# First heads of attention through memory, half by half, and a rearranged projection on five engines

## The chip, the cores and the metric

One core of a Trainium2 chip runs the whole program. The metric is the device time of one execution in microseconds, lower is better; the time of a version is the median of several executions. The engines are TensorE (PE, with its weight loads as PEld), VectorE (DVE), ScalarE (ACT), GpSimd (POOL) and SyncE (SP), which issues most DMAs. SPq is its queue of issues.

## What is computed

The program computes a macaron block: half a mixture-of-experts layer, attention, and half a mixture-of-experts layer again, on x of 4 x 1024 tokens by 256 features. The attention has 16 heads of 16 features, is causal, and adds a second product to the scores:

```
Q, K, V = heads(norm(x))                       # 16 heads of 16
scores = Q K' / 4 + lambda * (tanh(Q) J) tanh(K)'
out    = softmax(causal(scores)) V
x      = x + out Wo' + bo
```

The change is in the part between the first mixture and the attention, in which Q, K, V and the tangent terms of the first sequence are projected.

## The kernel before

Attention works in 16 groups: 4 sequences by 4 groups of heads (GH = 4 heads of HD = 16 features). A group's operands are two tiles, `a_qp` and `a_kp`, of 96 partitions (rows) by 4 heads by 1024 tokens, and `a_vg`. The 96 rows hold high and low parts of Q, K and the tangent terms, so that one product of TensorE gives a nearly exact float32 score.

`project` prepares the first sequence, before `attend`. It has four stages `STAGES` = (half 0, g 0), (half 1, g 0), (half 0, g 1), (half 1, g 1); a half is 512 tokens (QC), g picks 128 of the 256 features (two groups of heads, "sides" 0 and 1). x_hi and x_lo are the high and low part of the transposed normalized x. Each stage n does, in an order that is written out by hand for every engine:

- TensorE `queries(n)` and `keys(n)`, 6 products of 512 columns each, and `tangents(n)`, 3 products, from tanh of the queries (tq_hi, tq_lo).
- ScalarE `queries_high`, `keys_high` (three activations each: high part, tanh, high part of tanh) and `tangents_high`.
- VectorE `queries_low`, `keys_low`, `tangents_low`; GpSimd makes the low part of tanh(K) in all stages (L1379), and of tanh(Q) in stages 2 and 3 (L1377). VectorE makes that of tanh(Q) in stages 0 and 1 (L1435).
- The results go to `pack[n]`, 8 arrays of 128 partitions by 512 tokens, in the order Q_HI, T_HI, Q_LO, T_LO, K_HI, TK_HI, K_LO, TK_LO.

SP issues in program order and stands still at each wait. For stages 0 and 1 `load_heads_directly` (L1271) copies each array of side 0 from the 64 partitions of `pack` to 16 partitions of `a_qp` or `a_kp`, 12 DMAs of 128 KB for a half, 24 in all, each released by the array that is made last. `send_pack` (L1202) writes 4 arrays of one side, 512 KB, to `packs` in memory; the side 1 arrays of both halves go there after the last direct load. Then follow the values, the packs of stage 2, and in `attend` the loads of group 1 from `packs` (L1250), its values (L1256) and the packs of stage 3.

In `attend`, `max_unit` (L2289) computes score blocks whose row maximum VectorE takes (L2060, L2063), 48 units for a group. The first waits for the first heads (`heads_in`, L2284), the first of group 1 for all loads of group 1 (`loaded[1]`, L2286). After six units TensorE turns the next half of x. After the second unit of group 1 VectorE reduces group 0's maxima; they are turned, negated and sent as row 97 of `a_qp` by a DMA, and only then the first `score` (L2323) can run.

In the same stage VectorE also does the statistics of x (`statistics`, L146: 4 + 4 + 8 + 16 tiles) and ScalarE the square roots, whose table of functions differs from that of tanh.

`keep_running` (L1268) are TensorE products without use, put where it would otherwise be idle.

Of the kernel before, what the change touches and what calls it, by code (L numbers as in the profile page):

```python
# [5 lines left out]
F32 = mybir.dt.float32  # L6
# [3 lines left out]
ALU = mybir.AluOpType  # L10
# [1267 lines left out]
Q_ROWS = {Q_HI: (0, 4 * HD), T_HI: (HD, 5 * HD), Q_LO: (2 * HD,), T_LO: (3 * HD,)}  # L1278
K_ROWS = {K_HI: (0, 2 * HD), TK_HI: (HD, 3 * HD), K_LO: (4 * HD,), TK_LO: (5 * HD,)}
DIRECT_LOADS = sum(len(to) for rows in (Q_ROWS, K_ROWS) for to in rows.values())  # L1280


def project(kit, c, passing, proj, sum_dram, packs, v_dram, group, group_in):
# [8 lines left out]
    with ExitStack() as ctx:  # L1292
# [5 lines left out]
        pack += [sb(f"pack{u}", [P, 8, QC], F32R)[:] for u in range(FIRST_LATER, n_stages)]  # L1298
        vals = [proj["vals"], sb("vals1", [P, NG, U, GH, HV])]
# [11 lines left out]
         y_done, high_q, high_k, high_t, low_q, low_k, low_pool, low_tq, low_t, t_done, v_done, v_read, side_out, late_out) = kit.sems_until(  # L1311
            passing, "q", "stats_done v_ready root_ready root_done deviated normed tposed x_hi_done x_lo_done w_high w_low "
            "y_done high_q high_k high_t low_q low_k low_pool low_tq low_t t_done v_done v_read side_out late_out")
# [8 lines left out]
        def sync(sp):  # L1322
# [15 lines left out]
            for n, (i, g) in enumerate(STAGES):  # L1338
                if n == n_stages - 1:
                    continue  # L1340
                if n == 2:
                    for half in range(FIRST_LATER):
                        sp.wait_ge(v_ready, 3 + (half + 1) * U)
                        send_values(sp, v_dram, vals[half], half, v_out[half])
                if g == 0:
                    sp.wait_ge(low_q, n + 1)
                    load_heads_directly(sp, group[0], pack[n], i, (Q_HI, Q_LO), Q_ROWS, landed)
                    sp.wait_ge(low_k, n + 1)
                    load_heads_directly(sp, group[1], pack[n], i, (K_HI, K_LO), K_ROWS, landed)
                    sp.wait_ge(low_pool, 2 + n + 1)  # L1350
                    load_heads_directly(sp, group[1], pack[n], i, (TK_HI, TK_LO), K_ROWS, landed)
                    sp.wait_ge(low_t, n + 1)
                    load_heads_directly(sp, group[0], pack[n], i, (T_HI, T_LO), Q_ROWS, landed)
                    if n == FIRST_LATER - 1:
                        for half in range(FIRST_LATER):
                            send_pack(sp, packs, pack[half], half, g, slice(K_HI, 8), side_out, (1,))
                            send_pack(sp, packs, pack[half], half, g, slice(0, K_HI), side_out, (1,))
                else:
                    sp.wait_ge(low_k, n + 1)
                    sp.wait_ge(low_pool, 2 + n + 1)  # L1360
                    send_pack(sp, packs, pack[n], i, g, slice(K_HI, 8), late_out)
                    sp.wait_ge(low_t, n + 1)
                    send_pack(sp, packs, pack[n], i, g, slice(0, K_HI), late_out)
        def gpsimd(pool):
# [9 lines left out]
            for n in range(n_stages):  # L1374
                if n >= FIRST_LATER:
                    pool.wait_ge(high_q, 3 * n + 3)
                    nc.gpsimd.tensor_tensor(tq_lo[n % 2][:], tq[n % 2][:], tq_hi[n % 2][:].bitcast(F32), ALU.subtract).then_inc(low_tq, 1)  # L1377
# [29 lines left out]
        def vector(dve):  # L1407
# [17 lines left out]

            def x_rest(i):
# [3 lines left out]

            def queries_low(n):
                i, g = STAGES[n]
                dve.wait_ge(high_q, 3 * n + 3)
                if n < FIRST_LATER:
                    nc.vector.tensor_tensor(tq_lo[n % 2][:], tq[n % 2][:], tq_hi[n % 2][:].bitcast(F32), ALU.subtract).then_inc(low_tq, 1)  # L1435
# [26 lines left out]
            norm(1)  # L1462
            dve.wait_ge(w_low, 3)
            queries_low(0)
            x_rest(1)
# [16 lines left out]
        def scalar(act):  # L1482
# [20 lines left out]
            def queries_high(n):  # L1503
# [4 lines left out]
                if n > 1:  # L1508
                    act.wait_ge(low_tq, n - 1)
# [31 lines left out]
            roots(act, U, BT, 2)  # L1541
            norm(1)
# [3 lines left out]
            x_high(1)  # L1546
# [11 lines left out]
        def tensor(pe):  # L1558
# [27 lines left out]
            def keys(n):  # L1586
                i, g = STAGES[n]
                if n == 0:
                    pe.wait_ge(w_low, 2)
                else:  # L1590
                    pe.wait_ge(low_q, n)
# [3 lines left out]
            def tangents(n):  # L1595
# [6 lines left out]
                pe.wait_ge(low_tq, n + 1)  # L1602
# [22 lines left out]
            transposes(1)  # L1625
            tangents(0)
            queries(1)
# [34 lines left out]
def attend(kit, c, proj, sum_dram, packs, v_dram, o_dram, inv_dram, wo_dram, bo_dram, group, group_in):  # L1662
# [18 lines left out]
    with ExitStack() as ctx:  # L1681
# [124 lines left out]
        def sync(sp):  # L1806
# [28 lines left out]
            sp.wait_ge(heads_in, FIRST_LATER * DIRECT_LOADS * 16)  # L1835
# [80 lines left out]
        def gpsimd(pool):  # L1916
# [6 lines left out]
            pool.wait_ge(heads_in, FIRST_LATER * DIRECT_LOADS * 16)  # L1923
# [291 lines left out]
        def tensor(pe):  # L2215
# [65 lines left out]
            def max_unit(n, h, z):  # L2281
                qt, first, tiles_in = UNITS[z]
                if n == 0 and (h, z) == (0, 0):
                    pe.wait_ge(heads_in, FIRST_LATER * DIRECT_LOADS * 16)  # L2284
# [209 lines left out]
```

## Time and profile before

| what | value |
|---|---|
| median of 3 runs | 1550.21 us (1548.02 to 1551.75) |
| profiled execution, device time | 1552.77 us |
| its span | 1551.0 us, 25160 instructions |
| mean granted TensorE clock | 0.957 of full |
| projection stage (this change) | about 425.5 to 472.0 us of the span |
| attention | about 474 to 1110 us |

The span is the time from the first to the last instruction; 1.8 us of the device time lie around it. All stages run one after the other, so a microsecond that the change moves at the start of attention is a microsecond of the whole if nothing behind it has slack. A granted clock of 1.00 is 2.4 GHz, 0.50 is 1.2 GHz.

### The profile page before, as it was taken

How to read it: one execution, taken by the hardware profiler on the slowest of the kernel's cores; microseconds unless marked ns; L12 is line 12 of the kernel's file. 1: busy time of each engine (PE TensorE's matmuls, PEld its weight loads, DVE VectorE, ACT ScalarE, POOL GpSimd, SP SyncE). 2: the span in 40 equal slices, each digit the busy share in tenths (PEclk: the TensorE clock that was granted, in tenths of full speed). 3: DMA queues.
4: the chain of work that ended last, by engine and by line, in shares of the span. 5: the costliest groups of instructions: out<-in, count | busy, mean ns of one | idle time of the engine just before them, and what ended most of it. 6: DMA issues, size and time to landing. Idle time of an engine off the chain costs nothing. (4 is left out here: it accounts for less than half of the span.)

```text
span 1551.0 us, 25160 instructions
## 1 busy us (share of the span) xinstructions
PE 1437.4 (93%) x8872; PEld 1091.9 (70%) x8874; DVE 994.4 (64%) x2526; ACT 719.2 (46%) x1106; POOL 681.1 (44%) x654
## 2 busy tenths in 40 slices
PE   4699999999878899999999999999896999999998
PEld 3589889899866555555555555555565998898998
DVE  7756655555368576777777677886367566565554
ACT  5333333333263455555556565665473333333332
POOL 1365565664435442323333332225303655656644
PEclk9799999999989698989999999999987999999999
DMA  9454433442299866665656569562073444335432
GB/s 306 139 105 100 94 64 87 102 93 38 29 194 273 263 185 157 168 174 134 178 149 178 131 177 258 170 188 97 30 236 116 105 98 97 60 92 103 94 38 26
DMA packets 125509, 206.48 MB, mean 133 GB/s; under 512 B 24280, under 2 KB 86232, under 8 KB 122520
## 3 DMA queue, kind: packets, MB, share of 16 engines
q1 hardware_dynamic: 89032, 157.96, 36.3%
q0 software_dynamic: 30720, 38.46, 15.1%
q10 hardware_dynamic: 5648, 8.66, 1.9%
q8 instruction: 62, 1.02, 0.3%
q14 instruction: 47, 0.39, 0.1%
HBM read 123.22 MB, written 82.54 MB: 133 GB/s over the span
## 5 line engine op out<-in xcount | busy, mean ns | idle before, releaser
L2188 ACT ACTIVATE a_wts<-a_s_psum 128x1024 f32<-128x1024 f32 (+1 forms) x384 | 301.7, 810 | 218.3 <-PE a_s_psum L2323 216.3
L2060 DVE CUSTOM_DVE_ANT_0 a_m_psum<-a_m_psum,mask 128x256 f32<-128x256 f32 (+2 forms) x492 | 248.4, 519 | 140.7 <-PE a_m_psum L2289 130.4
L2289 PE MATMUL a_m_psum<-a_kp,a_qp 96*128 96x512 f32 (+1 forms) x735 | 275.9, 403 | 26.1 <-DVE a_parts L2060 17.4
L2289 PEld LDWEIGHTS a_m_psum<-a_kp,a_qp 96*128 96x128 f32 x735 | 142.4, 196 | 159.5 <-DVE a_parts L2060 81.0
L1997 POOL TENSOR_SCALAR_AFFINE_SELECT a_wts<-a_wts 128x512 f32<-128x512 f32 x128 | 78.2, 634 | 329.0 <-ACT a_wts L2188 328.8
L1032 ACT ACTIVATE e_act_a<-e_a_psum 128x512 f32<-128x512 f32 (+1 forms) x192 | 101.2, 527 | 259.4 <-PE e_a_psum L1111 259.4
L2323 PE MATMUL a_s_psum<-a_qp,a_kp 97*128 97x512 f32 (+2 forms) x768 | 213.8, 361 | 0.7 <-DMA a_qp<-stats 0.4
L949 DVE TENSOR_TENSOR e_hid<-e_act_a,e_g_psum 128x512 f32<-128x512 f32 (+1 forms) x192 | 114.7, 597 | 141.5 <-PE e_g_psum L1111 136.8
L243 POOL DMA_INDIRECT e_slots<-normalized,e_token x160 | 166.2, 1039 | 81.7 <-issue 47.5
L1130 PE MATMUL e_o_psum<-e_w_hi,e_h_hi 128*128 128x256 f32 x640 | 183.4, 287 | 0.0
L890 POOL DMA_INDIRECT out<-e_res,e_sum_row x80 | 126.5, 1582 | 126.5 <-ACT e_res L1044 113.1
L890 POOL DMA_INDIRECT sums<-e_res,e_sum_row x80 | 126.5, 1581 | 126.1 <-ACT e_res L1044 104.9
L1130 PE MATMUL e_o_psum<-e_w_hi,e_h_lo 128*128 128x256 f32 x640 | 181.0, 283 | 0.0
L1130 PE MATMUL e_o_psum<-e_w_lo,e_h_hi 128*128 128x256 f32 x640 | 181.0, 283 | 0.0
L2063 DVE TENSOR_REDUCE a_parts<-a_m_psum 128x1 f32<-128x512 f32 x243 | 159.2, 655 | 10.5 <-PE a_m_psum L2289 7.0
L2339 PE MATMUL a_o_psum<-a_wts,a_vg 128*17 128x512 f32 (+3 forms) x1536 | 159.8, 505 | 4.0 <-POOL a_wts L1997 2.7
L2323 PEld LDWEIGHTS a_s_psum<-a_qp,a_kp 97*128 97x128 f32 x768 | 136.5, 195 | 19.0 <-ACT a_wts L2188 4.7
L1044 ACT ACTIVATE e_res<-e_o_psum,e_gate 128x256 f32<-128x256 f32 x160 | 75.9, 475 | 147.7 <-PE e_o_psum L1130 147.7
L1111 PE MATMUL e_a_psum<-e_s_hi,e_w_hi 128*128 128x512 f32 (+1 forms) x384 | 139.3, 363 | 5.4 <-DVE e_s_lo L929 2.8
L1111 PE MATMUL e_a_psum<-e_s_lo,e_w_hi 128*128 128x512 f32 (+1 forms) x384 | 136.0, 354 | 0.0
L1111 PE MATMUL e_a_psum<-e_s_hi,e_w_lo 128*128 128x512 f32 (+1 forms) x384 | 136.0, 354 | 0.0
L1111 PE MATMUL e_g_psum<-e_s_hi,e_w_hi 128*128 128x512 f32 (+1 forms) x384 | 135.9, 354 | 0.0
(292 smaller groups left out, 2702.9 us busy)
## 6 DMA issues: line engine op xcount, KB each, us to landing
packs<-x_res SPq DMA_DIRECT2D x48, 512.0 KB, 5.9
e_w_raw<-in_W_in SPq DMA_DIRECT2D x16, 1024.0 KB, 6.6
a_qp<-packs SPq DMA_DIRECT2D x15, 1024.0 KB, 8.0
a_kp<-packs SPq DMA_DIRECT2D x15, 1024.0 KB, 14.0
e_w_raw<-in_W_out SPq DMA_DIRECT2D x16, 512.0 KB, 8.4
normalized<-r_xn SPq DMA_DIRECT2D x16, 512.0 KB, 4.4
attended<-a_o_sb ACTq DMA_DIRECT2D x32, 256.0 KB, 4.6
a_qp<-packs SPq DMA_DIRECT2D x15, 512.0 KB, 10.1
```

Of the source, the lines that this page charges most:

```text
L243: pool.indirect_dma_start(held["slots"][e % 2][:, j * ROW:(j + 1) * ROW], None, xn_dram, bass.IndirectOffsetOnAxis(ap=held["token"][:, at: ...
L890: nc.gpsimd.indirect_dma_start(sum_dram, bass.IndirectOffsetOnAxis(ap=sum_row[:, at:at + 1], axis=0), res[j][:], None, bounds_check=last_r ...
L949: nc.vector.tensor_tensor(hid[q][:, 0:n], act_a[q][:, 0:n], g_ps[q][:, 0:n], ALU.mult).then_inc(hid_done, 1)
L1032: nc.scalar.activation(act_a[q][:, 0:n], a_ps[q][:, 0:n], ACT.Gelu).then_inc(gelu_done, 1)
L1111: last = nc.tensor.matmul(bank[q][:, 0:n], w_in_at(w, k, half + f), s[:, k, c0:c0 + n], start=(z == 0), stop=(z == len(terms) - 1))
L1130: last = nc.tensor.matmul(o_ps[(u * ST + c0 // P + j) % 2][:, 0:D], s[:, k, j * P:(j + 1) * P], w_out_at(w, k), start=(z == 0), stop=(z == ...
L2060: nc.vector.tensor_tensor_reduce(products, products, c["mask"][:, QC - width:], 1.0, MASKED, ALU.add, ALU.max, top).then_inc(max_read, 1)
L2063: nc.vector.reduce_max(top, products, AX.X).then_inc(max_read, 1)
L2188: nc.scalar.activation(wts[(u * NS + s) % 2][:, j, 0:w], s_ps[q % 2][:, 0:w], ACT.Exp).then_inc(weighed, 1)
L2289: nc.tensor.matmul(m_ps[bank((n, h, z))][:, 0:stream], qp[n % NB][0:PACK, h, qt * P:(qt + 1) * P], kp[n % NB][0:PACK, h, first * P:first * ...
L2323: last = nc.tensor.matmul(s_ps[q % 2][:, col - lead:col + w], kp[u][:, j, kt * P:(kt + 1) * P], qp[u][:, j, at - lead:at + w], start=True, ...
L2339: last = nc.tensor.matmul(o_ps[j * HP:j * HP + HV, q0:q0 + w], vg[u][:, kt, j, :], wts[(u * NS + s) % 2][:, j, col:col + w], start=(kt == ...
```

## The change

Its short description also says that statistics stand in other places; in the diff no call of `statistics` is moved, only the calls around them. What the diff does:

1. The 24 direct loads are gone. For each half SP writes side 0 of the pack to memory (two DMAs of 512 KB), waits until both have landed (`first_out`), and reads it back with four DMAs (`load_first_heads`) to 32, 64, 64 and 32 partitions. Arrays K are now sent first, Q second. The side 1 packs follow after the second half's loads, as before.
2. VectorE makes x_hi of half 1 (`second_x_high`, two copies from PSUM), which ScalarE did between `queries_high(0)` and `keys_high(0)`.
3. VectorE makes tq_lo in all stages (`turned_low`), GpSimd none. `low_tq` becomes part of `low_q`. In stage 0 it now stands ahead of the wait for `w_low`, `second_x_high` and `x_rest(1)`.
4. ScalarE does one tanh of a single column right after its second square root, ahead of `norm(1)`.
5. TensorE runs `queries(1)` ahead of `tangents(0)`.

```diff
-def load_heads_directly(eng, tile, pack, half, arrays, rows, sem):
-    for a in arrays:
-        for to in rows[a]:
-            eng.dma_start(tile[to:to + HD, :, half * QC:(half + 1) * QC].bitcast(F32), pack[0:HALF, a, :].bitcast(F32)).then_inc(sem, 16)
+def load_first_heads(eng, group, packs, half, sem):
+    qp, kp, _ = group
+    rows = packs.rearrange("n a (r j) c -> n (a r) j c", j=GH)[0, :, :, half * QC:(half + 1) * QC]
+    for t, to, at, n in ((kp, 0, 4 * HD, 2 * HD), (kp, 2 * HD, 4 * HD, 4 * HD), (qp, 0, 0, 4 * HD), (qp, 4 * HD, 0, 2 * HD)):
+        eng.dma_start(t[to:to + n, :, half * QC:(half + 1) * QC].bitcast(F32), rows[at:at + n, :, :]).then_inc(sem, 16)
...
                 if g == 0:
-                    sp.wait_ge(low_q, n + 1)
-                    load_heads_directly(sp, group[0], pack[n], i, (Q_HI, Q_LO), Q_ROWS, landed)
                     sp.wait_ge(low_k, n + 1)
-                    load_heads_directly(sp, group[1], pack[n], i, (K_HI, K_LO), K_ROWS, landed)
                     sp.wait_ge(low_pool, 2 + n + 1)
-                    load_heads_directly(sp, group[1], pack[n], i, (TK_HI, TK_LO), K_ROWS, landed)
+                    send_pack(sp, packs, pack[n], i, g, slice(K_HI, 8), first_out, (0,))
+                    sp.wait_ge(low_q, 2 * n + 2)
                     sp.wait_ge(low_t, n + 1)
-                    load_heads_directly(sp, group[0], pack[n], i, (T_HI, T_LO), Q_ROWS, landed)
-                    if n == FIRST_LATER - 1:
+                    send_pack(sp, packs, pack[n], i, g, slice(0, K_HI), first_out, (0,))
+                    sp.wait_ge(first_out, (n + 1) * 2 * 16)
+                    load_first_heads(sp, group, packs, i, landed)
+                    if n == 1:
...
-                if n >= FIRST_LATER:
-                    pool.wait_ge(high_q, 3 * n + 3)
-                    nc.gpsimd.tensor_tensor(tq_lo[n % 2][:], ...).then_inc(low_tq, 1)
...
+            def second_x_high():
+                dve.wait_ge(tposed, 2)
+                for k in range(KD):
+                    nc.vector.tensor_copy(x_hi[1][:, k, :], tp[:, k, :]).then_inc(x_hi_done, 1)
...
             norm(1)
+            dve.wait_ge(high_q, 3)
+            turned_low(0)
+            second_x_high()
+            x_rest(1)
             dve.wait_ge(w_low, 3)
             queries_low(0)
-            x_rest(1)
...
             roots(act, U, BT, 2)
+            nc.scalar.activation(unread[:], rstd[:, 0:1], ACT.Tanh)
             norm(1)
...
             queries_high(0)
-            x_high(1)
             keys_high(0)
...
             transposes(1)
+            queries(1)
             tangents(0)
-            queries(1)
             keys(1)
```

## Rows read from the trace of the kernel before

**Rows 1.** The page's first part: busy time of an engine, share of the span.
```profile
PE 1437.4 (93%) x8872; PEld 1091.9 (70%) x8874; DVE 994.4 (64%) x2526; ACT 719.2 (46%) x1106; POOL 681.1 (44%) x654
```

**Rows 2.** Table by stretch: busy us of each engine, granted clock, DMA share, GB/s.
```profile
441.00:442.00 1.00, 0.95 (x9) 0.86 (x8) 0.00 (x0) 0.98 (x3) 0.00 (x0) 1.00 1.10 349
...
448.00:451.00 3.00, 3.00 (x9) 2.32 (x8) 0.30 (x1) 1.17 (x3) 0.22 (x1) 0.50 1.07 126
...
474.20:477.00 2.80, 2.78 (x13) 2.44 (x14) 2.49 (x9) 1.53 (x4) 0.00 (x0) 0.72 1.05 406
...
520.00:530.00 10.00, 9.07 (x29) 5.28 (x29) 6.27 (x18) 2.97 (x6) 6.57 (x9) 0.50 0.95 234
```

**Rows 3.** TensorE in order of time: start, us, instruction, [idle before, releaser].
```profile
441.15 1.06 PE L1573 MATMUL q_tp_psum<-ident,q_stage 128*128 128x128 f32 x8
445.10 0.77 PE L1564 MATMUL q_t_psum<-q_tq_hi,q_w_hi 128*128 128x512 f32 x1 [2.88 <-DVE q_tq_lo L1435]
...
458.05 0.47 PE L1564 MATMUL q_t_psum<-q_tq_hi,q_w_hi 128*128 128x512 f32 x1 [1.20 <-POOL q_tq_lo L1377]
...
462.93 0.47 PE L1564 MATMUL q_t_psum<-q_tq_hi,q_w_hi 128*128 128x512 f32 x1 [2.33 <-POOL q_tq_lo L1377]
...
474.22 0.74 PE L2289 MATMUL a_m_psum<-a_kp,a_qp 96*128 96x256 f32 x3 [2.22 <-DMA a_qp<-q_pack]
...
500.50 0.49 PE L2289 MATMUL a_s_psum<-a_kp,a_qp 96*128 96x512 f32 x1
504.99 0.58 PE L2289 MATMUL a_m_psum<-a_kp,a_qp 96*128 96x256 f32 x1 [3.99 <-DMA a_vg<-values]
...
513.87 1.33 PE L2323 MATMUL a_s_psum<-a_qp,a_kp 97*128 97x512 f32 x3 [0.43 <-DMA a_qp<-stats]
```

**Rows 4.** SP's queue in order of time: issues of DMAs, start, us, count.
```profile
459.21 1.88 SPq L1275 DMA_DIRECT2D a_qp<-q_pack  x3
...
561.89 1.12 SPq L1250 DMA_DIRECT2D a_qp<-packs  x2
...
599.68 1.12 SPq L1250 DMA_DIRECT2D a_qp<-packs  x2
...
644.08 1.12 SPq L1250 DMA_DIRECT2D a_qp<-packs  x2
...
956.65 1.11 SPq L1250 DMA_DIRECT2D a_qp<-packs  x2
```

**Rows 5.** DMA landing, us from issue: issues in 445.5:446.3, in 663.9:664.6 and in 958.4:959.1.
```profile
a_qp<-q_pack SPq DMA_DIRECT2D x1, 128.0 KB, 3.5
...
packs<-x_res SPq DMA_DIRECT2D x1, 512.0 KB, 4.6
...
a_kp<-packs SPq DMA_DIRECT2D x1, 1024.0 KB, 13.8
```

**Rows 6.** ScalarE in order of time, stage 0.
```profile
441.59 1.28 ACT L1510 ACT_TABLE_LOAD   x1
...
444.04 1.07 ACT L1501 CAST q_x_hi<-q_tp_psum 128x512 fp32r<-128x512 f32 x2
```

**Rows 7.** VectorE in order of time, stages 0 to 2 and the start of group 1.
```profile
438.34 0.94 DVE L203 SCALAR_TENSOR_TENSOR q_tmp<-q_tmp 128x4 f32<-128x4 f32 x1
439.32 0.16 DVE L204 TENSOR_TENSOR q_tmp<-q_tmp 128x4 f32<-128x4 f32 x1
...
444.25 0.69 DVE L1435 TENSOR_TENSOR q_tq_lo<-q_tq,q_tq_hi 128x512 fp32r<-128x512 f32 x1 [3.61 <-ACT q_tq_hi L1513]
...
445.53 1.28 DVE L1429 TENSOR_TENSOR q_x_lo<-q_tp_psum,q_x_hi 128x512 fp32r<-128x512 f32 x2
...
455.52 2.70 DVE L146 BATCH_NORM_STATS2 stats<-x_res 128x6 f32<-128x256 f32 x8
...
505.76 0.30 DVE L2060 CUSTOM_DVE_ANT_0 a_m_psum<-a_m_psum,mask 128x128 f32<-128x128 f32 x1 [2.25 <-PE a_m_psum L2289]
```

**Rows 8.** GpSimd in order of time, beside the row at 438.34.
```profile
437.25 2.01 POOL L1373 TENSOR_TENSOR q_w_lo<-q_w_raw,q_w_hi 128x256 fp32r<-128x256 f32 x2 [7.81 <-ACT q_w_hi L1489]
```

More of the change, by code:

```diff
@@ L1268, in keep_running @@
         pe.matmul(out[:, 0:P], c["ident"][:], c["ident"][:], start=True, stop=True)
-def load_heads_directly(eng, tile, pack, half, arrays, rows, sem):
-    for a in arrays:
-        for to in rows[a]:
-            eng.dma_start(tile[to:to + HD, :, half * QC:(half + 1) * QC].bitcast(F32), pack[0:HALF, a, :].bitcast(F32)).then_inc(sem, 16)
-Q_ROWS = {Q_HI: (0, 4 * HD), T_HI: (HD, 5 * HD), Q_LO: (2 * HD,), T_LO: (3 * HD,)}
-K_ROWS = {K_HI: (0, 2 * HD), TK_HI: (HD, 3 * HD), K_LO: (4 * HD,), TK_LO: (5 * HD,)}
-DIRECT_LOADS = sum(len(to) for rows in (Q_ROWS, K_ROWS) for to in rows.values())
+def load_first_heads(eng, group, packs, half, sem):
[3 more added lines that the diff above has]
+        eng.dma_start(t[to:to + n, :, half * QC:(half + 1) * QC].bitcast(F32), rows[at:at + n, :, :]).then_inc(sem, 16)
+FIRST_LOADS = 4
 def project(kit, c, passing, proj, sum_dram, packs, v_dram, group, group_in):
@@ L1298, in project @@
         pack += [sb(f"pack{u}", [P, 8, QC], F32R)[:] for u in range(FIRST_LATER, n_stages)]
+        unread = sb("unread", [P, 1])
         vals = [proj["vals"], sb("vals1", [P, NG, U, GH, HV])]
@@ L1310, in project @@
         (stats_done, v_ready, root_ready, root_done, deviated, normed, tposed, x_hi_done, x_lo_done, w_high, w_low,
-         y_done, high_q, high_k, high_t, low_q, low_k, low_pool, low_tq, low_t, t_done, v_done, v_read, side_out, late_out) = kit.sems_until(
+         y_done, high_q, high_k, high_t, low_q, low_k, low_pool, low_t, t_done, v_done, v_read, first_out, side_out, late_out) = kit.sems_until(
             passing, "q", "stats_done v_ready root_ready root_done deviated normed tposed x_hi_done x_lo_done w_high w_low "
-            "y_done high_q high_k high_t low_q low_k low_pool low_tq low_t t_done v_done v_read side_out late_out")
+            "y_done high_q high_k high_t low_q low_k low_pool low_t t_done v_done v_read first_out side_out late_out")
         v_out = kit.sems_until(passing, "q_v_out", "0 1")
@@ L1374, in gpsimd @@
             for n in range(n_stages):
-                if n >= FIRST_LATER:
-                    pool.wait_ge(high_q, 3 * n + 3)
-                    nc.gpsimd.tensor_tensor(tq_lo[n % 2][:], tq[n % 2][:], tq_hi[n % 2][:].bitcast(F32), ALU.subtract).then_inc(low_tq, 1)
                 pool.wait_ge(high_k, 3 * n + 3)
@@ L1429, in x_rest, with turned_low @@
                     nc.vector.tensor_tensor(x_lo[i][:, k, :], tp[:, k, :], x_hi[i][:, k, :].bitcast(F32), ALU.subtract).then_inc(x_lo_done, 1)
+            def turned_low(n):
+                nc.vector.tensor_tensor(tq_lo[n % 2][:], tq[n % 2][:], tq_hi[n % 2][:].bitcast(F32), ALU.subtract).then_inc(low_q, 1)
             def queries_low(n):
@@ L1433, in queries_low @@
                 dve.wait_ge(high_q, 3 * n + 3)
-                if n < FIRST_LATER:
-                    nc.vector.tensor_tensor(tq_lo[n % 2][:], tq[n % 2][:], tq_hi[n % 2][:].bitcast(F32), ALU.subtract).then_inc(low_tq, 1)
+                if n:
+                    turned_low(n)
                 nc.vector.scalar_tensor_tensor(pack[n][:, Q_LO, :], y_ps[2 * n % NY][:], bias[:, 2, g:g + 1], pack[n][:, Q_HI, :].bitcast(F32),
@@ L1590, in keys @@
                 else:
-                    pe.wait_ge(low_q, n)
+                    pe.wait_ge(low_q, 2 * n)
                 split_product(y_ps[(2 * n + 1) % NY][:], [(wt(a, 1, k, g * P, P), b[i][:, k, :]) for k in range(KD)
@@ L1601, in tangents @@
                     pe.wait_ge(low_t, n)
[L1602 removed]
+                pe.wait_ge(low_q, 2 * n + 1)
                 split_product(t_ps[:], [(jt(w_hi, g), tq_hi[n % 2][:]), (jt(w_hi, g), tq_lo[n % 2][:]),
@@ L1834, in sync @@
                 sp.wait_ge(done, n)
-            sp.wait_ge(heads_in, FIRST_LATER * DIRECT_LOADS * 16)
+            sp.wait_ge(heads_in, FIRST_LATER * FIRST_LOADS * 16)
             sp.wait_ge(proj["side_out"], FIRST_LATER * 2 * 16)
```

6 lines of the change are left out of this document (3 added, 3 removed).

## The prediction

> **What bounds the kernel now.** The page's first part comes first: TensorE is busy 93% of the span [rows 1], an average that says nothing of the 50 us that the change touches. So I read TensorE in order of time around them and look for its idle time and what ended it. In the projection it waits for tq_lo: 2.88 us in stage 0, 1.20 and 2.33 us in stages 2 and 3 [rows 3]. Then it stands 2.22 us until 474.22, released by the last direct load, and 3.99 us until 504.99, released by the last load of group 1; the first score starts at 513.87, behind group 0's maxima, which are complete only after the second unit of group 1 [rows 3]. Everything in attention follows from these two DMA waits. What ends last is therefore the queue of DMAs and not an engine. The table by stretch shows why: from 448 us on the DMA engines are fully busy and move only 126 GB/s, while the writes of packs right after 474 run at 406 GB/s [rows 2]. The 24 direct loads are 24 x 128 KB = 3.15 MB, and 3.15 MB in the 26 us from 448 to 474.2 is 120 GB/s: they fill the whole stage. The last three are issued from 459.21 [rows 4] and land about 13 us later, so they wait in the queue and not for an engine.
>
> From 474.2 the queue is still full: side 1 packs 2.1 MB, values 1.1 MB, packs of stage 2 2.1 MB, group 1's loads 3.4 MB. It takes 504.99 - 474.22 = 30.8 us until group 1 is there [rows 3]. That stretch keeps its length whenever it starts, since all of it is ready and issued earlier. **So the change is worth what it does to the moment when the first heads are complete (474.2 now).**
>
> **Part 1, when the heads can leave.** The change of order on five engines decides when stage 0's arrays are ready. Tanh's table is loaded before norm(1), where ScalarE waits anyway, so tq_hi is ready 1.28 us sooner [rows 6]: VectorE's tq_lo of stage 0, which started at 444.25 on that release, starts at 442.97 and ends after 0.69 us at 443.65 [rows 7]. The x_hi copies go from ScalarE (1.07 us for two [rows 6]) to VectorE. VectorE's copy out of PSUM isn't in the trace; between ScalarE's 0.54 each and the 0.64 of VectorE's own pass over the same tile [rows 7] I take 0.6, so 1.2, and x_lo 1.28: complete at 446.1. Before it was 446.8, from 445.53 [rows 7]. queries(1) thus starts 0.7 us earlier, at 446.1. But TensorE has been idle since its turns ended at 442.2 [rows 3]. It now idles 3.9 us, not 2.88, and as before it comes back at the low clock (granted 0.50, 1.2 GHz [rows 2]): 512 columns at 1.2 GHz are 0.43 us. queries(1) takes 6 x 0.43 = 2.6 us and tangents(0) 3 x 0.43 = 1.3 us, until 450.0. T_HI and T_LO add 0.7 + 0.75: the Q pack of half 0 leaves at 451.4. The K pack went at about 447.5 and is under way. tangents(0), moved behind, costs nothing on ScalarE but time: it ends 3 us later than before, and queries_high(1), queued behind tangents_high(0) on ScalarE, starts at 450.7 where queries(1) alone would allow 448.8. Stage 1 ends about 0.5 us later than now, near 456. Half 1's packs don't care: SP is still busy with half 0 then.
>
> **Part 2, the way through memory.** Removed: 24 x 128 KB at 120 GB/s, 26 us of the DMA engines. Added: 2.1 MB written and 3.15 MB read, and, twice, a wait of SP until the writes have landed.
> - A write of 512 KB to memory with little before it lands 4.6 us after issue [rows 5]. Half 0's Q pack: 451.4 + 4.6 = 456.0.
> - A read-back of a half is 1.57 MB. The nearest row is a whole group's loads into the same partitions: first issue 956.65 [rows 4], last landing about 958.5 + 13.8 = 972.3 [rows 4, 5], 15.6 us for 3.15 MB and a store of 0.26 MB beside them. The fixed part is about 2.4 us: a lone 128 KB load took 3.5 us [rows 5], and 1.1 of it are its bytes at 120 GB/s. So (15.6 - 2.4) x 3.15/3.41/2 + 2.4 = 8.5 us. The other end: 349 GB/s, the rate of loads into all 128 partitions [rows 2], gives 1.57/0.349 = 4.5 + 2.4 = 6.9 us. I take 8.5, since these loads write 32 and 64 partitions, as the group's do.
> - Half 0 is back at 456.0 + 8.5 = 464.5. SP is free after its four issues at 458.5 and sends half 1's two packs, but they stand behind the loads: 1.05 MB at 406 GB/s [rows 2] are 2.6 us more, 467.1. Then the second read-back: 467.1 + 8.5 = **475.6**, against 474.2. The change is **+1.3 us** here.
> - Bounds: with 3.5 us for the write (the least landing of rows 5) and 6.9 for the reads, 451.4 + 3.5 + 6.9 + 2.6 + 6.9 = 471.3, 2.9 us less than now. With nothing of the attended store taken out of the reads (9.05 each) and the second write not overlapped at all (4.6 + 0.6), 451.4 + 4.6 + 9.05 + 5.2 + 9.05 = 479.3, 5.1 us more.
>
> The Trainium skill, "SBUF — State Buffer", section "Door 1: The DMA port swizzle", says that a DMA's rate goes by how many of 16 SBUF ports its partitions reach: 16 partitions reach 4 of them (about 109 GB/s), and 0..63 no more than 0..31 (about 218 GB/s). The direct loads, into 16 partitions, agree at 126 [rows 2]. For packs out of 64 partitions it would make the write 4.8 instead of 2.6 us and the heads later by 2.2, an estimate from the page; here the row speaks against the page, for side 1 packs leave 64 partitions at 406 GB/s [rows 2]. For the read-back it supports the dearer of my two ends.
>
> **Part 3, what else moves.** SP passes the waits for first_out with the side 1 packs and the values queued behind: they are issued from about 470 instead of 461. That costs nothing as long as the first heads are still flowing (until 475.6); if the cover went, it would be the gap itself, some 2 us. GpSimd loses two subtractions; VectorE does them in 0.69 us, but it is in order behind statistics of 2.70 us, started at 455.52 [rows 7], now at about 456.1. So tq_lo(2) comes at 459.5 rather than 457.9, which was TensorE's release at 458.05 [rows 3], and stage 2 loses 1.4 us; stage 3 gives most of it back, for its 2.33 us wait [rows 3] has a shorter release. The stage ends 0.5 to 1.5 us later and with it the norm of the next half, at 475.4 now. The x turn comes after six units, 1.3 us behind the heads' landing: 476.9. That hides it. The tanh of one column is 0.2 us in idle time.
>
> VectorE's tq_lo reads two tiles of SBUF next to GpSimd's low part of tanh(K). A row shows what that can cost: a subtraction-like step of 0.16 us took 0.94 while GpSimd ran from 437.25 to 439.26 [rows 7, 8]. At worst tq_lo(2) waits for the 1.3 us of GpSimd's step, and the x turn has 476.9 - 476.4 = 0.5 us left. The Trainium skill, "SBUF — State Buffer", section "Who interferes with whom", calls this an exclusive lock of a shared pair of ports; the trace agrees, and the sum stands.
>
> **Rivals.**
> 1. *The read-back is fast.* Heads at 471.3. Against it: the group rows; for it: 349 GB/s. Then the queue lets group 1 in at 502.1, and VectorE, which now waits 2.25 us for that unit [rows 7], is the bound: gain 2.3 us. TensorE's 3.99 us of idle at 501 to 505 [rows 3] go, and with them possibly the low clock that follows (0.50 in 520 to 530 [rows 2]). Group 0 takes 561.89 - 513.87 = 48.0 us to its last mix, group 2 takes 644.08 - 599.68 = 44.4 [rows 3, 4]: 3.6 more. 1550.2 - 5.9 = **1544.3**.
> 2. *The round trip is the new wait* (slower). SP waits for two writes in series with two reads, and the DMA engines idle meanwhile. It decides from heads later than 477.3 (+3.1). At the upper bound, 479.3, all of attention starts 5.1 us later: **1555.3**. For it: 9 us is measured for like bytes; against it: writes right behind reads overlap.
> 3. *The heads were not the bound, the projection is.* If heads land by 473 and the norm is 1.5 us late, the x turn and VectorE's chain of maxima bind, and the gain in DMA time is lost to the later stage: + 0.8, **1551.0**. This is also the case in which the change does less than it says.
>
> **How the numbers follow.** Forecast: own profiled time 1552.77 + 1.3 = 1554.1; that run lies 2.56 above the median, so 1550.21 + 1.3 = 1551.5. Chances: forecast (heads 472.5 to 477.3) 0.42, rival 1 0.27, rival 2 0.21, rival 3 0.10. A measurement tells about 0.2% (3.1 us) from no change: faster 0.27, same 0.52, slower 0.21. The range takes in rival 1's time and nearly the upper bound: 1544.5 to 1555.
>
> **What would show it.** The DMA rows of 448 to 474: gaps with no traffic at 450, 456 and 467 and rates of 200 to 400 GB/s between. The release of the first unit (now 474.22), of group 1 (504.99) and the first score (513.87), each later by the same 1.3. The read-back's landing: 8.5 us from first issue; at 7 rival 1 holds. The clock after 505. I am wrong if the heads come before 472 or after 477.3, or if the 30.8 us behind them change length.

## The result: the change makes the kernel half a percent slower

| | before | after |
|---|---|---|
| median of 20 runs each | 1545.34 us (1540.36 to 1552.11) | 1552.32 us (1546.33 to 1561.23) |
| ratio | | 1.0048, 95% interval 1.0033 to 1.0064 |
| profiled execution, span | 1551.0 us | 1549.1 us |

The change costs 0.48%, 7.4 us of 1545 (7.0 between the medians); forecast were 1551.5 us and +1.3 us, in a range up to 1555. The single profiled executions say the opposite (1549.1 against 1551.0); both lie within the runs' spread, and further down it is seen where the trace of after makes up its delay. The stage that the change touches must be read from the traces, the total from the medians.

TensorE of the kernel after, in order of time: start, us, instruction, idle before and its releaser. They are the counterparts of [rows 3].
```profile
434.60 1.09 PE L1581 MATMUL q_tp_psum<-ident,q_stage 128*128 128x128 f32 x8 [1.22 <-ACT q_stage L1503]
...
445.92 0.80 PE L1572 MATMUL q_y_psum<-q_x_hi,q_w_hi 128*128 128x512 f32 x1 [3.69 <-DVE q_x_lo L1431]
...
459.26 0.48 PE L1572 MATMUL q_t_psum<-q_tq_hi,q_w_hi 128*128 128x512 f32 x1 [2.07 <-DVE q_tq_lo L1434]
...
463.54 0.47 PE L1572 MATMUL q_t_psum<-q_tq_hi,q_w_hi 128*128 128x512 f32 x1 [1.92 <-DVE q_tq_lo L1434]
...
478.56 1.22 PE L2297 MATMUL a_m_psum<-a_kp,a_qp 96*128 96x256 f32 x3 [5.86 <-DMA a_qp<-packs]
...
511.38 0.58 PE L2297 MATMUL a_m_psum<-a_kp,a_qp 96*128 96x256 f32 x1 [5.53 <-DMA a_vg<-values]
...
520.51 1.33 PE L2331 MATMUL a_s_psum<-a_qp,a_kp 97*128 97x512 f32 x3 [0.68 <-DMA a_qp<-stats]
```
The first turns of x in the projection stand at the same place in both (434.6), so the positions compare directly. The first heads are used at 478.56, 4.3 us later than at 474.22. Group 1 is there at 511.38, 6.4 us later, and the first score starts at 520.51, 6.6 us later. So 6.6 of the 7.4 us of the medians are there when the scores start.

SP's queue of the kernel after (start, us, DMAs issued), the counterpart of [rows 4], and then the one line of the kernel before that now matters, its first load of group 1.
```profile
447.21 5.09 SPq L1206 DMA_DIRECT2D packs<-q_pack  x2
456.00 2.01 SPq L1276 DMA_DIRECT2D a_kp<-packs  x2
458.05 1.26 SPq L1276 DMA_DIRECT2D a_qp<-packs  x2
459.41 1.40 SPq L1206 DMA_DIRECT2D packs<-q_pack  x2
468.44 1.22 SPq L1276 DMA_DIRECT2D a_kp<-packs  x2
469.70 1.26 SPq L1276 DMA_DIRECT2D a_qp<-packs  x2
471.00 4.28 SPq L1206 DMA_DIRECT2D packs<-q_pack  x4
475.33 9.68 SPq L1214 DMA_DIRECT2D values<-q_vals  x8
485.52 5.70 SPq L1206 DMA_DIRECT2D packs<-q_pack  x4
491.62 3.32 SPq L1250 DMA_DIRECT2D a_qp<-packs  x2
```
```profile
484.62 2.96 SPq L1250 DMA_DIRECT2D a_qp<-packs  x2
```
SP stands still from 452.3 to 456.0 and from 460.8 to 468.4, waiting for its own writes. What is queued behind, the side 1 packs, comes at 471.0. Group 1's loads are issued at 491.62 instead of 484.62.

How busy the DMA engines are in the kernel after: a table by stretch (busy us of each engine, clock, DMA share, GB/s), the counterpart of [rows 2].
```profile
450.00:451.00 1.00, 1.00 (x4) 0.81 (x3) 0.11 (x1) 0.83 (x2) 0.00 (x0) 0.50 0.99 213
...
452.00:453.00 1.00, 1.00 (x6) 0.82 (x5) 0.38 (x1) 1.00 (x3) 0.00 (x0) 1.00 0.05 12
...
465.00:466.00 1.00, 1.00 (x10) 0.98 (x9) 0.95 (x3) 0.65 (x3) 1.00 (x2) 1.00 1.05 393
...
468.00:469.00 1.00, 1.00 (x11) 1.00 (x10) 1.00 (x4) 0.48 (x2) 0.95 (x2) 1.00 0.00 0
...
474.00:475.00 1.00, 0.00 (x0) 0.00 (x0) 0.41 (x1) 1.00 (x3) 0.20 (x2) 1.00 0.93 205
...
486.00:487.00 1.00, 1.00 (x6) 0.79 (x5) 1.00 (x3) 0.98 (x2) 1.00 (x1) 1.00 0.25 74
```
The gaps at 452 and 468 are the two waits. At 486 there is a third gap, and SP waits for nothing in it: the eight issues of the values have taken it 9.68 us, and the queue has run dry before the packs of stage 2 are issued at 485.52.

Why the profiled execution of after is not longer than that of before: the granted clock in the later groups, after's table by stretch first, then before's.
```profile
600.00:610.00 10.00, 8.57 (x60) 4.76 (x61) 7.16 (x22) 4.88 (x8) 1.10 (x2) 1.00 0.70 158
...
850.00:860.00 10.00, 9.04 (x53) 5.05 (x52) 5.84 (x17) 4.87 (x11) 3.34 (x6) 1.00 0.87 257
```
```profile
600.00:610.00 10.00, 8.23 (x34) 5.92 (x33) 7.67 (x21) 5.93 (x9) 1.81 (x3) 0.76 0.94 218
...
850.00:860.00 10.00, 9.52 (x35) 5.66 (x34) 4.79 (x13) 3.46 (x7) 1.81 (x3) 0.66 0.90 263
```
Before had stretches at a lower clock at 600 to 620 and 850 to 860 that this execution of after didn't have. How the delay shrinks meanwhile is seen in SP's first loads of the later groups, here those of after:
```profile
567.02 1.12 SPq L1250 DMA_DIRECT2D a_qp<-packs  x2
...
645.82 1.12 SPq L1250 DMA_DIRECT2D a_qp<-packs  x2
...
884.70 1.12 SPq L1250 DMA_DIRECT2D a_qp<-packs  x2
```
The loads of before stand at 561.89, 644.08 [rows 4] and 887.08: after is 5.1 us late, then 1.7 late, then 2.4 early. Of these 7.5 us 5.3 go between the two loads on either side of the two stretches; the rest, and the 1.5 us that are gone before 562, I can't place. The two profiles don't have such stretches in the same places; that the runs' spread of some 10 us comes from there is likely, but no run isolates it.

### The profile page after: what moved, and what is told of

Same layout as the page of the kernel before. It is cut to its first block and busy times, and to the rows that moved or that the text cites. A ratio compares the mean times of both kernels' runs of the same rounds, so it can differ in the third digit from the quotient of the medians.

```text
span 1549.1 us, 25153 instructions
## 1 busy us (share of the span) xinstructions
PE 1426.0 (92%) x8872; PEld 1084.0 (70%) x8874; DVE 996.1 (64%) x2530; ACT 718.1 (46%) x1105; POOL 680.9 (44%) x652
## 3 DMA queue, kind: packets, MB, share of 16 engines
q0 software_dynamic: 30720, 38.46, 15.1%
## 6 DMA issues: line engine op xcount, KB each, us to landing
a_qp<-packs SPq DMA_DIRECT2D x17, 512.0 KB, 10.1
```

## The experiments

All but the first two rows of this table were run later, the rows e on one chip and the rows c and d on a second, where the kernel before takes about 1565 us, so totals are given as ratios to the kernel before on the same chip, and positions in us from the first turns of x in each trace (434.6 above). "Group 1 issued" is the first load of group 1 on SP's queue. e4 and d1 put wrong operands into the first group's scores and serve only for measuring.

| kernel | heads used | group 1 issued | first score | ratio to before (95%) |
|---|---|---|---|---|
| before | 39.6 | 50.0 | 79.3 | 1 |
| after | 44.0 | 57.0 | 85.9 | 1.0048 (1.0033, 1.0064) |
| c1 before again | 39.5 | 49.8 | 78.6 | 1.0005 (0.9974, 1.0036) |
| c2 after again | 44.2 | 58.4 | 86.3 | 1.0050 (1.0025, 1.0074) |
| e1 trip only | 43.3 | 58.2 | 86.2 | 1.0065 (1.0027, 1.0102) |
| e2 engines only | 41.7 | 52.0 | 81.5 | 1.0026 (0.9994, 1.0059) |
| e3 values from GpSimd | 43.3 | 52.9 | 82.5 | 1.0039 (1.0008, 1.0069) |
| e4 no wait for writes | 37.6 | 49.2 | 78.5 | 0.9982 (0.9950, 1.0014) |
| c3 packs in two | 43.4 | 56.6 | 85.4 | 1.0052 (1.0031, 1.0074) |
| c4 keys from GpSimd | 39.2 | 49.6 | 80.1 | 1.0024 (0.9996, 1.0051) |
| d1 direct to 32 rows | 37.0 | 48.1 | 76.0 | 0.9972 (0.9945, 0.9999) |
| d2 keys, queries apart | 39.0 | 54.2 | 81.9 | 1.0047 (1.0024, 1.0070) |
| d3 one read-back | 42.5 | 57.1 | 86.1 | 1.0063 (1.0025, 1.0100) |
| d4 apart, values moved | 38.3 | 52.1 | 80.7 | 1.0022 (1.0001, 1.0042) |

**The kernel before and the kernel after once more, beside the others.**

> The kernel before, unchanged, for a trace from the same chip as the runs beside it. Every theory expects its heads complete about 40 us after the first turns of x in the projection and group 1 some 31 us after the heads, at the absolute times of this chip.

> The changed kernel, unchanged, on the same chip as the kernel before. Theory (what the profiles show, 6.4 us at the first score): heads 4 to 5 us later than in the run of the kernel before beside it, group 1 some 2 us more, total 0.3 to 0.6% slower. Rival (the difference of the two first profiles is chance): heads and group 1 within 1 us.

Both repeat themselves within 1.4 us in every column of the table, and the ratio is 1.0050 after 1.0048. The difference of the two first profiles in this stage is not chance.

**Which part of the change costs: e1, the trip through memory alone.**
```diff
 # the kernel before, with load_first_heads, first_out and the new SP order; all else as before
-                    load_heads_directly(sp, group[0], pack[n], i, (Q_HI, Q_LO), Q_ROWS, landed)
+                    send_pack(sp, packs, pack[n], i, g, slice(K_HI, 8), first_out, (0,))
...
+                    sp.wait_ge(first_out, (n + 1) * 2 * 16)
+                    load_first_heads(sp, group, packs, i, landed)
```


> The kernel before with part 1 of the change alone: side 0 of each half is written to memory, SP waits for both writes, four loads read it back; the order on the other engines is that of before. Theory (the round trip through memory is the new wait): heads complete about 4 us later than the 474.2 of before, group 1 about 6 us later than 505.0, total +5 to +8 us. Rival (the rearrangement of the engines costs the time): heads within 1 us of 474.2 and total within 2 us of before.

```profile
487.20 1.22 PE L2288 MATMUL a_m_psum<-a_kp,a_qp 96*128 96x256 f32 x3 [5.00 <-DMA a_qp<-packs]
```
This is TensorE's first unit in its trace, 43.3 us after the turns at 443.90. The trip alone makes the first score as late as the whole change does (86.2 against 86.3), as the theory expected. Group 1 is there 8.0 us later than in c1, where I had expected 6, and the ratio 1.0065 is 10 us where I had expected 5 to 8, which its interval includes.

**e2, the engines' rearrangement alone.**
```diff
 # the kernel after, with the direct loads back
-                    sp.wait_ge(first_out, (n + 1) * 2 * 16)
-                    load_first_heads(sp, group, packs, i, landed)
+                    load_heads_directly(sp, group[0], pack[n], i, (Q_HI, Q_LO), Q_ROWS, landed)
...
```


> The changed kernel with the 24 direct loads put back (in their old order, with their old waits), so that only the engines' rearrangement is left. Theory: the DMA engines are full from 448 us either way at 120 GB/s, so the heads complete at 474 plus or minus 1 and the total is within 2 us of before, although tq_lo(2) comes about 1.2 us later. Rival (the rearrangement is to blame): +4 us or more.

```profile
487.35 1.22 PE L2298 MATMUL a_m_psum<-a_kp,a_qp 96*128 96x256 f32 x3 [4.66 <-DMA a_qp<-q_pack]
```
Heads at 41.7, 2.2 us later than in c1; I had expected at most 1. SP's first direct loads, in before and in e2:
```profile
445.64 1.97 SPq L1275 DMA_DIRECT2D a_qp<-q_pack  x3
```
```profile
457.63 1.96 SPq L1275 DMA_DIRECT2D a_qp<-q_pack  x3
```
In e2 the first is issued 11.9 us after the turns (457.63 against 445.69), before's 11.05 (445.64 against 434.59): queries_low(0) now stands behind x_hi and x_lo on VectorE. That is 0.9 us of the 2.2; for the rest, the same 24 loads take 29.7 us from the first issue to the heads where c1 has 28.4, and why I can't say. The interval of the ratio, 1.0026, includes no change. So the rearrangement buys nothing and probably costs a little; it isn't where the 7 us are, since e1 without it has them all.

**e4, no wait for the writes.**
```diff
-                    sp.wait_ge(first_out, (n + 1) * 2 * 16)
-                    load_first_heads(sp, group, packs, i, landed)
+                    load_first_heads(sp, group, sum_dram.rearrange("(n a p r) d -> n a p (r d)", n=2, a=8, p=GH * HD), i, landed)
```


> The changed kernel without SP's wait for first_out: the read-back has the same shapes and bytes but reads the array of sums instead of packs, so that it needs no write (the first heads' scores of sequence 0 are computed from wrong operands; all writes are still made). Theory (the two waits in series are what costs; the DMA engines' own work of 5.2 MB is about 17 us): heads complete at 468 to 471, 8 to 10 us before those of the changed kernel, and group 1 at 502 or earlier. Rival (the read-back's rate into 32 and 64 partitions is what costs): heads within 3 us of 478.5.

```profile
483.59 0.73 PE L2296 MATMUL a_m_psum<-a_kp,a_qp 96*128 96x256 f32 x3 [0.43 <-DMA a_qp<-sums]
```
Same bytes, same DMAs, no waits: heads 6.6 us sooner than in c2, with only 0.43 us of waiting left, and the ratio falls from 1.0050 to 0.9982. The intervals don't touch, so the two waits in series are what the change loses by. Group 1 comes 69.6 us after the turns, where c2 has 77.9. Both positions are a little short of what I expected (8 to 10 us sooner, and 67).

The same trace shows what I had overlooked, the next events on TensorE behind the heads:
```profile
486.64 1.06 PE L2260 MATMUL a_m_psum<-ident,x_res 128*128 128x128 f32 x8 [1.74 <-DVE a_parts L2067]
...
515.63 0.58 PE L2296 MATMUL a_m_psum<-a_kp,a_qp 96*128 96x256 f32 x1 [4.12 <-DMA a_vg<-values]
...
524.53 1.33 PE L2330 MATMUL a_s_psum<-a_qp,a_kp 97*128 97x512 f32 x3 [0.45 <-DMA a_qp<-stats]
```
With the waits gone the heads are 1.9 us sooner than in c1, the kernel before, but TensorE then waits 1.74 us for VectorE ahead of the turn of x, group 1 comes at 69.6 (c1 69.5) and the first score at 78.5 (78.6). Even without the waits the trip only draws level with the direct loads.

**e3, the values from another queue.**
```diff
-                if n == 2:
-                    for half in range(FIRST_LATER):
-                        sp.wait_ge(v_ready, 3 + (half + 1) * U)
-                        send_values(sp, v_dram, vals[half], half, v_out[half])
...
+            for half in range(FIRST_LATER):
+                pool.wait_ge(v_ready, 3 + (half + 1) * U)
+                send_values(nc.gpsimd, v_dram, vals[half], half, v_out[half])
```


> The changed kernel, but the 8 DMAs of the first sequence's values are issued from GpSimd's queue and not from SP's, where they take 9.7 us of issuing. Theory (behind the later heads SP can't feed the DMA queue: in the changed kernel's trace it moves 74 GB/s at 486 to 487 and 214 at 482 to 483, and group 1 comes 32.8 us after the heads, not 30.8): heads still at 478.5, but group 1 at most 31 us after them, total 2 to 4 us below the changed kernel. Rival (the stretch is longer because the DMA engines themselves need longer): 32 to 33 us, no gain.

SP's queue in its trace:
```profile
478.83 14.54 SPq L1206 DMA_DIRECT2D packs<-q_pack  x8
495.58 2.19 SPq L1250 DMA_DIRECT2D a_qp<-packs  x2
```
and the first unit of group 1 on TensorE:
```profile
515.99 0.48 PE L2296 MATMUL a_m_psum<-a_kp,a_qp 96*128 96x256 f32 x1 [1.30 <-DMA a_vg<-values]
```
The heads come 0.9 us sooner than in c2, group 1 comes 30.0 us after them and no longer 33.7, and the first score 3.8 us sooner. The bytes are the same, so the longer stretch is SP's late feeding, not the DMA engines' work. The total, 1.0039 against 1.0050, moved the right way, but far within its interval: the gain is shown in the stage, not in the total.

**c3, each pack in two DMAs.**
```diff
-                    send_pack(sp, packs, pack[n], i, g, slice(K_HI, 8), first_out, (0,))
+                    send_pack(sp, packs, pack[n], i, g, slice(K_HI, K_LO), first_out, (0,))
+                    send_pack(sp, packs, pack[n], i, g, slice(K_LO, 8), first_out, (0,))
```


> The changed kernel, but each pack of side 0 that is written for the first heads goes as two DMAs of 256 KB issued one after the other, not as one of 512 KB. A lone pack moved at 205 GB/s in the changed kernel's trace, two in a row at 393. If one DMA alone can't fill the engines, two halves run at up to 390 GB/s and the Q pack of half 0 lands about 1 us sooner. If the rate is that at which one queue's descriptors are made, or that of the 64 partitions it is read from, the rate stays near 205 and the landing stays 4.3 to 4.7 us after the first issue (plus up to 0.6 for the second issue).

The rates by stretch stay at 215 and 201 GB/s in the microseconds from 461 and 465, and SP reaches the read-back 21.4 us after the turns, as in the kernel after. Splitting doesn't help: writes that enter an empty queue ran at some 205 GB/s, one or two at a time (e1's pair too, 195 to 227), and those that stand behind a backlog at up to 393 (the line from 465 to 466 above).

**d1, what limits the direct loads.**
```diff
-        for to in rows[a]:
-            eng.dma_start(tile[to:to + HD, :, half * QC:(half + 1) * QC].bitcast(F32), pack[0:HALF, a, :].bitcast(F32)).then_inc(sem, 16)
+        for to in rows[a]:
+            at, heads = to // HD % 3 * 2 * HD, to // HD // 3 * 2
+            eng.dma_start(tile[at:at + 2 * HD, heads:heads + 2, half * QC:(half + 1) * QC].bitcast(F32), pack[0:HALF, a, :].bitcast(F32)).then_inc(sem, 16)
```


> The kernel before, but each direct load of 128 KB writes 32 partitions of two heads' columns and not 16 partitions of four heads' (same source, same bytes, same count; the rows land in wrong places, so the first group's scores are computed from wrong operands). If the 120 GB/s of the direct loads come from writing only 16 partitions, the rate rises to about 200 GB/s, the heads are there about 30 us after the first turns of x and TensorE no longer waits for them (39.5 us in the kernel before). If copying from tile to tile, or 128 KB per DMA, is the limit, the rate stays at 120 GB/s and the heads at 39 to 40 us.

The kernel before with its bytes going to 32 partitions, table by stretch (last two columns: DMA share and GB/s; one line of it below): 154 to 166 GB/s from 463 to 477, the engines full, where c1 (the second line) moved 109 to 129 in the same part of the stage.
```profile
470.00:471.00 1.00, 1.00 (x5) 0.83 (x6) 0.80 (x2) 0.98 (x2) 0.67 (x1) 1.00 1.03 164
```
```profile
468.00:470.00 2.00, 0.43 (x2) 0.41 (x3) 0.90 (x2) 1.82 (x4) 1.38 (x2) 1.00 1.07 126
```
The width of the target is part of the limit, but not all of it: twice the partitions gave 1.3 times the rate, not the 1.7 times that I expected. TensorE no longer waits for the heads (37.0), the first score comes 2.6 us sooner than in c1, and the ratio 0.9972 is the best of all. It isn't a usable kernel, since a copy from 64 rows to 16 is what the layout asks for.

**c4, direct loads from two queues.**
```diff
 # e2, with the 12 direct loads of the key tile issued on GpSimd after its low part of tanh(K)
+                if n < FIRST_LATER:
+                    pool.wait_ge(low_k, n + 1)
+                    load_heads_directly(nc.gpsimd, group[1], pack[n], STAGES[n][0], (K_HI, K_LO), K_ROWS, keys_landed)
...
```


> Direct loads as in the kernel before, on the changed kernel's order of engines, but the 12 direct loads of the key tile are issued from GpSimd's queue while SP issues those of the query tile. If what limits direct loads is that one DMA at a time writes 16 partitions (120 GB/s), two queues side by side reach up to twice that, the heads are complete 5 to 8 us earlier than with one queue, the wait for group 1 shrinks and the total is 3 to 7 us below the kernel before. If the DMA engines are the limit whatever they write to, or GpSimd's own descriptor making is, the heads come at the same time or later and the total stays or rises.

With both queues at work the rate stays between 96 and 145 GB/s from 461 to 481, and only then rises:
```profile
470.00:471.00 1.00, 0.38 (x2) 0.37 (x3) 1.00 (x2) 0.00 (x0) 0.99 (x2) 1.00 1.13 135
```
Two queues don't add up. TensorE doesn't wait for the heads here (39.2 is when it comes to them), so they were in a little sooner than in e2, but the total, 1.0024, is that of e2 (1.0026). A gain of 3 to 7 us on the kernel before, which I had hoped for, is excluded.

**d2, keys and queries apart.**
```diff
+                    send_pack(sp, packs, pack[n], i, g, slice(K_HI, 8), first_k, (0,))
+                    if n == 1:
+                        sp.wait_ge(first_q, 16)
+                        load_first_queries(sp, group, packs, 0, landed)
...
+                    sp.wait_ge(first_k, (n + 1) * 16)
+                    load_first_keys(sp, group, packs, i, landed)
```


> The changed kernel, but SP waits for the key pack and for the query pack apart: while the queries' write is under way the keys are read back, and half 1's key pack is sent before half 0's queries are read. All bytes and DMAs are the same. Theory (the waits in series leave the DMA engines idle, some 10 us of the stage): heads 36 to 40 us after the first turns of x instead of 44, total 0.2 to 0.6% below the changed kernel, near or below the kernel before. Rival (the read-back itself is the cost, 10 us for a half whenever it runs): heads at 42 us or later.

SP's queue in its trace:
```profile
478.48 6.29 SPq L1206 DMA_DIRECT2D packs<-q_pack  x4
484.81 7.95 SPq L1214 DMA_DIRECT2D values<-q_vals  x8
493.28 6.27 SPq L1206 DMA_DIRECT2D packs<-q_pack  x4
499.95 3.32 SPq L1250 DMA_DIRECT2D a_qp<-packs  x2
```
This is the run that I learned most from. The heads come 5 us sooner than in c2 (39.0), and nobody waits for them any more. Yet the ratio is 1.0047. SP is still held by the last of its waits, the side 1 packs go out only 32.7 us after the turns (before: 26.5), and at 494 to 495 the DMA engines move next to nothing. TensorE waits once more, now for VectorE ahead of the turn of x, and then for group 1:
```profile
494.00:495.00 1.00, 1.00 (x6) 0.77 (x5) 0.96 (x3) 0.98 (x2) 0.99 (x1) 1.00 0.07 14
```
```profile
488.34 1.94 PE L2274 MATMUL a_m_psum<-ident,x_res 128*128 128x128 f32 x8 [2.21 <-DVE a_parts L2081]
...
518.81 0.58 PE L2310 MATMUL a_m_psum<-a_kp,a_qp 96*128 96x256 f32 x1 [5.00 <-DMA a_vg<-values]
```
Group 1 is there 34.0 us behind the heads. Against the kernel before (c1) the heads are 0.5 us sooner and group 1 is 3.5 us later: early heads alone don't bring group 1. Against c2 group 1 is 4.9 us and the first score 4.3 us sooner. The total doesn't show that, but it doesn't exclude it either: with these two intervals (1.0024 to 1.0070 and 1.0025 to 1.0074) the difference of the ratios is uncertain by some 0.3%, about 5 us.

**d3, one read-back for both halves.**
```diff
-                    sp.wait_ge(first_out, (n + 1) * 2 * 16)
-                    load_first_heads(sp, group, packs, i, landed)
-                    if n == 1:
+                    if n == 1:
+                        sp.wait_ge(first_out, 2 * 2 * 16)
+                        load_queries_and_keys(sp, group, packs, 0, landed)
```


> The changed kernel, but both halves are written first, with one wait, and read back with the four DMAs that every other group uses (rows of 16 KB, 3.15 MB). It takes one round trip out of the chain. The group loads of later groups take 15 to 16 us; half 1's write lands about 26 us after the first turns of x, so the heads come at 41 to 43 us. If a read-back in runs of 2 KB (10.1 us for a half in the changed kernel) is slow because of its 768 short runs, this one with 4 us fewer per MB lands by 40 us; if it is bound by the partitions it writes, at 41 to 43.

```profile
486.49 1.04 PE L2297 MATMUL a_m_psum<-a_kp,a_qp 96*128 96x256 f32 x3 [3.60 <-DMA a_kp<-packs]
```
Heads at 42.5, inside the 41 to 43 that I expected for a read bound by the partitions it writes: 15.1 us from the issue at 471.38 for twice the bytes of a half, which took 10.1 us in runs of 2 KB. The 40 us or less of the other case didn't come. One round trip less gains 1.7 us at the heads and nothing at the first score (86.1) or in the total.

**d4, both remedies.** The edits of d2 and of e3 together.

> As the kernel with keys and queries apart, and the values' 8 DMAs issued from GpSimd's queue. Theory (two costs that add up: the serial waits, and SP's late feeding of the DMA queue): heads 36 to 40 us after the first turns of x, group 1 at most 31 us after them, total 0 to 0.5% below the kernel before. Rival (the values' place doesn't matter once the heads are early): the same total as with SP issuing them, within 0.1%.

Heads at 38.3, group 1 at 71.4 and so 33.1 us behind them (expected at most 31), first score at 80.7, ratio 1.0022 with 1.0001 as its lower end. The first score recovers 5.6 of the 7.7 us between c1 and c2, the ratio about half of the loss; the kernel before is not reached. The rival (same total as d2) isn't excluded, for the intervals overlap. No usable version of this study beats the kernel before.

**What the table says as a whole.** From "group 1 issued" to "first score" it is 29.3, 28.9, 28.8, 27.9, 28.0, 29.5, 29.6, 29.3, 28.8, 30.5, 27.9, 27.7, 29.0 and 28.6 us, row by row. From "heads used" to the first score it is between 39.0 and 43.6. The first number is the steadier (2.8 us of spread against 4.6): the start of the scores goes with the moment when SP comes to issue group 1's loads more than with the first heads. And the totals go with the start of the scores. In the order of their first scores the rows have the ratios 0.9972 (d1, 76.0), 0.9982 (e4, 78.5), 1.0005 (c1, 78.6), 1 (before, 79.3), 1.0024 (c4, 80.1), 1.0022 (d4, 80.7), 1.0026 (e2, 81.5), 1.0047 (d2, 81.9), 1.0039 (e3, 82.5), 1.0052 (c3, 85.4), 1.0048 (after, 85.9), 1.0063 (d3, 86.1), 1.0065 (e1, 86.2) and 1.0050 (c2, 86.3). Few neighbours are told apart by their intervals, but the row as a whole rises.

## Why the prediction was right or wrong

The range held the time (1552.3 us in 1544.5 to 1555) and the direction was right; the size that I forecast is a fifth of the loss. That the time lies only 0.8 us from the forecast is luck: I added +1.3 us to the median of three runs, 1550.21, and the median of the 20 is 1545.34. These 4.9 us of a high start nearly make up for the 6 us by which the change was priced too low; from 1545.34 the same sum gives 1546.6 and its upper end 1550.1, and the measured time lies above both. The case that came true is rival 2, the round trip as the new wait, to which I gave 0.21 against 0.42 for the forecast: heads at 478.56, later than its 477.3. Its mechanism (two waits in series, DMA engines idle meanwhile) is what e4 shows. Its price, +5.1 us, was somewhat small.

1. **What bounds the kernel.** Right: both waits of TensorE are waits for DMAs and both grew (5.86 and 5.53 us, from 2.22 and 3.99 in [rows 3]).
2. **Part 1, when the heads can leave.** Right within 0.2 us in most steps. tq_lo(0) was forecast at 442.97 and started at 442.78; queries(1) at 446.1, it came at 445.92; the Q pack's landing at 456.0, it was 456.00. VectorE's two copies took 1.28 us, not 1.2:
```profile
442.78 0.69 DVE L1434 TENSOR_TENSOR q_tq_lo<-q_tq,q_tq_hi 128x512 fp32r<-128x512 f32 x1 [2.11 <-ACT q_tq_hi L1521]
443.39 1.28 DVE L1426 CAST q_x_hi<-q_tp_psum 128x512 fp32r<-128x512 f32 x2
444.58 1.28 DVE L1431 TENSOR_TENSOR q_x_lo<-q_tp_psum,q_x_hi 128x512 fp32r<-128x512 f32 x2
```
   What I left out: in stage 0 the direct loads of the kernel before start on queries_low(0), so for that kernel's path the rearrangement is a loss of 0.9 us (e2); the sum wasn't touched by it.
3. **Part 2, the read-back.** This term was mis-sized. I took 8.5 us for a half, scaled from whole groups. It was 10.1 us both times: from 456.00 until the last of four loads, issued at about 458.7, landed 7.4 us later, and from 468.44 until 470.3 plus 8.2. The landing lines, issues in 458.7:459.3 and in 470.3:470.95:
```profile
a_qp<-packs SPq DMA_DIRECT2D x1, 256.0 KB, 7.4
```
```profile
a_qp<-packs SPq DMA_DIRECT2D x1, 256.0 KB, 8.2
```
   Twice 1.6 us are 3.2, and the write behind the first read-back took 2.3, not 2.6. So the heads came 3.0 us later than forecast (478.56 against 475.6), all of it from this term. The scaling from a group to a half was the error: half the bytes took 10.1 of 15.1 us (d3), so the fixed share is probably larger than the 2.4 us that I subtracted (d3 reads in longer runs, so the two don't compare exactly); I had it from a lone load of 128 KB. Two slips carry nothing: the 9.05 us of the upper bound is 9.0 by its own rows, and the range, from 1544.5, doesn't quite take in rival 1's 1544.3.
4. **The 30.8 us behind the heads.** This assumption was wrong. I wrote that the stretch keeps its length because "all of it is ready and issued earlier". It is ready earlier, but issued on one queue behind SP's new waits, and it became 32.8 us. The gap at 486 is the cover of Part 3 that went. I had priced it correctly ("the gap itself, some 2 us") and then set it to nothing. e3 shows it: with 8 issues off SP's queue the stretch is 30.0. With the assumption falls the sentence built on it, that the change is worth what it does to the moment of the first heads. In e4 they come 1.9 us sooner than in c1 and in d2 0.5 sooner, and group 1 comes 0.1 and 3.5 us later. It fails in both directions: late heads cost more than their delay, and early ones bring nothing where SP doesn't come to group 1's loads sooner.
5. **Part 3, the rest.** tq_lo(2) was forecast at 459.5 as the release of the tangents of stage 2; they started at 459.26. In stage 3 the start was 463.54, 0.6 later than before. GpSimd's step next to VectorE's tq_lo(2) took 1.59 instead of 1.29 us, so working side by side cost 0.3 us of the 1.3 feared, and it cost GpSimd, not tq_lo(2) (0.67 us). None of this reached the end, as forecast.
```profile
458.67 1.59 POOL L1376 TENSOR_TENSOR q_pack<-q_tk,q_pack 128x512 fp32r<-128x512 f32 x1 [2.97 <-ACT q_pack L1531]
```
6. **The writes' rate.** I let the row decide (406 GB/s) against the Trainium skill, "SBUF — State Buffer", section "Door 1: The DMA port swizzle", whose rule gives 218 GB/s for 64 partitions. Both are seen here: 205 GB/s for packs into an empty queue, 393 for packs of the same shape, from the same 64 partitions, behind a backlog. Where 393 is measured the rule's 218 doesn't hold, and it can't alone be the reason for the lower rate. For the direct loads I said that the rule agrees; the measured 126 GB/s are 16% above the 109 that I quoted, so that was only roughly so. My sum used 4.6 us for the first write and 2.6 for the queued pair, and both held within 0.3.
7. **Rivals 1 and 3.** Rival 1 needed a read-back of 6.9 us; it was 10.1. Its clock gain didn't come either: the clock was at its lower level (0.50) from 510 to 535 in the kernel after, in the kernel before from 505 to 530. Nor does that stretch hang on the wait for group 1: in d4 this wait is down to 0.67 us, at 517.6, and the clock is 0.50 from 520 to 545 all the same. Rival 3's condition didn't arise, since the heads were later and not earlier; but where an experiment makes them early its mechanism is there: TensorE then waits ahead of the turn of x for VectorE, 1.74 us in e4, 2.21 in d2 and 2.42 in d1.

## What to carry to other kernels

Where one queue issues everything in program order, price a new wait not by what it waits for but by the transfer that stands last behind it and that an engine needs: here the loads of the next group, 7 us later. Replacing slow direct copies by a trip through memory trades DMA time for latency. Here the DMA engines were idle during the two waits, and even with the waits taken out (e4) the first score came no sooner than with the direct copies. And check by an experiment that removes only the wait (other data, same bytes) whether the engines' work or the wait is the price.

## What was unexpected in the hardware

- A write to memory into an empty queue ran at 205 GB/s and behind a backlog at 393 GB/s, same partitions and same 2 KB runs; splitting it in two changed nothing (c3). Why is open, and no run tests it.
- Copies from tile to tile into 16 partitions ran at 109 to 129 GB/s (c1, in steps of 2 us) with the DMA engines full, whether one or two queues issued them (c4: 96 to 145 in steps of 1 us), and into 32 partitions at 154 to 166 (d1).
- Two executions of the same program differ by 10 us and more, over 0.6%. With 12 runs the interval of a ratio is still 0.2 to 0.4% on either side, larger than the differences between most of these variants. The positions inside the stage repeated within 1.4 us and were the better instrument.
